# One load of the rotary weights ahead of the next phase's weights, and two weightings moved ahead of the step sizes at three sequences

## The chip, the cores and the metric

The kernel runs on one core of a Trainium2 chip. The time is that of the device, in microseconds (us), from one launch to its end; the median of several runs counts. A profiled execution gives the trace and has a time of its own.

## The reference, cut to what matters

The program is a decoder of four layers over `x` of 16 sequences, 128 rows each, 256 wide, all in float32. Each layer has a mixer or attention, a cross attention and a feed-forward part, each on a layer norm of `x` and added to `x`. Two of the twelve parts are touched.

The mixer of layer 2 (a state-space scan, 32 heads of 16, state 128):

```python
gate, hBC, dt = jnp.split(hidden @ in_proj_w.T, [INTER, INTER + CONV_DIM], axis=-1)
hBC = silu(causal_conv4(hBC, conv_w) + conv_b)
xs, B, C = jnp.split(hBC, [INTER, INTER + STATE], axis=-1)
dt = clip(softplus(dt + dt_bias), 0, 100)
# per head, causal: y[l] = sum over s <= l of
#     (C[l] . B[s]) * exp(sum of A*dt over s+1..l) * (dt[s] * xs[s])   + D * xs[l]
y = y * silu(gate)
return (y * rsqrt(mean(y * y) + EPS) * norm_w) @ out_proj_w.T
```

The cross attention of layer 2 (latent, 16 heads, 64 rotary columns each):

```python
kv_c, q_c = kv @ W_kvc, q @ W_dq
q_nope, q_rope = q_c @ W_uq, rope(q_c @ W_qr)
k_nope, k_rope, v = kv_c @ W_uk, rope(kv_c @ W_kr), kv_c @ W_uv
scores = (q_nope . k_nope + q_rope . k_rope) * scale, masked by seg_id
return softmax(scores) @ v @ W_o
```

`rope` swaps the two halves of the 64 columns for its second term, so the kernel keeps `W_qr` twice: as it is, and with the halves of each head swapped.

## The kernel before, in words

The twelve parts are phases that run one after another. Each phase is one or two blocks; a block has a program for each engine (`block.sync` for SP, which issues the loads, `block.gpsimd`, `block.tensor`, `block.scalar`, `block.vector`), and all engines meet at its end. Within a block the order on each engine is written out by hand, and engines wait for each other by semaphores. Weights of the next phase go into the other half of an arena `w`: the function `after(sp)`, made by `load_next`, issues them at the start of a phase.

**The mixer** (`mixer`, L1663; called for both layers with a mixer, with `PADDED` true only for the larger one of layer 2) treats the 16 sequences in 4 groups of 4 (`TG`). The vector engine's loop over sequences `q` weights the decays: `weigh(d)` (L2007, instruction at L2011) multiplies a tile of 8 heads x 128 x 128 decay factors by the similarity `gm`. In the larger mixer there are `PT` = 4 such tiles for a sequence, made in two pairs (`PU` = 2) by ScalarE's `decay` (L1860, an Exp at L1865), which waits for `exponents` on TensorE. TensorE's `outputs` (L2216) takes the weighted tiles one by one. `add(q)` (L2027) adds the projected result of the sequence before, `gated(q)` (L2022) takes the gate, `values(q)` (L1998) makes the scaled inputs. The work of the next group is woven in: after sequence `t` = 0 of a group come `step_bias` (L1939, adds the bias to the step-size product, then frees its PSUM bank), ScalarE's `softplus` (L1837 to L1841), two convolutions (`conv`, L1981; ScalarE's copies ahead of them at L1830 and L1832), and after `t` = 1 `step_sizes` (L1947 and behind). Products of that kind take turns in two PSUM banks, so the second convolution's product takes the bank that the step-size product had. These are the lines of the order before, on VectorE around a sequence with `t` = 0:

```python
for i in range(PT):
    weigh(PT * q + i)
    if q >= 1 and i == PU - 1:
        add(q - 1)
```

**The latent preparation** (`phase_xattn2`, L2819, first block) multiplies out the per-head weights on TensorE (L2914, L2919; ScalarE copies them out at L2932, L2935), normalises the first group, and splits the rotary weights into a rounded part `wh` (ScalarE, L2938) and the rest `wl` (VectorE, L2965). The split weights have three kinds of rows, `LAT`, `ROPE` and `SWAP`. SP issues, in this order: the next phase's weights (`in_l2f_up`, `in_l2f_down`), three copies of `in_l2x_qr` into `raw` (as it is, and each half into the place of the other), the segment numbers `seg`, and the first context tile. ScalarE and VectorE wait for all four small loads together, with one semaphore. The second block begins with TensorE's L3170 (which wants the context tile) and ScalarE's L3012 (which wants the next phase's weights).

## Time and profile before

| | |
|---|---|
| median of 3 runs | 2321.14 us (2319.14 to 2321.93) |
| the profiled execution | 2322.72 us, span 2320.9 us |
| mean granted TensorE clock | 0.947 |
| busy: TensorE, VectorE, ScalarE, GpSimd | 89%, 69%, 53%, 13% |
| loads `in_l2f_up`, `in_l2f_down` | 2048 KB and 1024 KB |
| loads `in_l2x_qr`: full, two halves | 384 KB, 192 KB each |
| loads `seg`, context tile | 8 KB, 512 KB |

The span runs from the first to the last instruction. A timeline line gives the start in us from the span's start, the duration in us of what was merged in the line, engine, line of the kernel, operation, output <- inputs, and in brackets how long the engine sat idle before it and what ended that. The granted clock is a share of 2.4 GHz: 1.00 is 2.4 and 0.50 is 1.2. Matmuls overlap each other, so that starts tell more of them than durations.

### The profile page before, as it was taken

Reading aid. Unit: us, or ns where it says so; the run is one execution under the profiler, and the core shown is the slowest. Engines: PE = TensorE matmul, PEld = TensorE weight load, DVE = VectorE, ACT = ScalarE, POOL = GpSimd, SP = SyncE. Lnnn points to the kernel's source line nnn. Section 1 sums busy time; section 2 is a strip of 40 time slices with the busy share of each in tenths; the row PEclk is TensorE's granted clock in tenths of the full one; section 3 lists DMA queues with packets and bytes.
Section 4 is the critical chain, followed back from the end, with each engine's and each line's share of the span. In section 5 each row is a group of like instructions: output and inputs, shape, how many; then the busy total and the mean of one; then the engine's idle time right before and its main releaser. Section 6 shows DMA issues by size and latency. Waiting matters only on the chain. (4 is left out here: it accounts for less than half of the span.)

```text
span 2320.9 us, 46693 instructions
## 1 busy us (share of the span) xinstructions
PE 2065.3 (89%) x18816; PEld 1575.8 (68%) x18816; DVE 1601.7 (69%) x2974; ACT 1237.4 (53%) x2455; POOL 302.0 (13%) x307
## 2 busy tenths in 40 slices
PE   7978989899899898888879898979889879999996
PEld 4644458677555787556657666758656658999996
DVE  5756657676465897777858877857566676766763
ACT  2325664544466444555546456565478524665663
POOL 0010000011310000001000000000100113444432
PEclk9978999899999999899989999999899879999998
DMA  3020010100100002000020000010200035666663
GB/s 120 22 66 23 14 44 1 37 1 1 60 20 24 12 1 72 1 1 1 1 78 10 9 18 0 0 37 1 73 2 2 7 120 184 207 193 221 197 206 89
DMA packets 62793, 126.10 MB, mean 54 GB/s; under 512 B 16073, under 2 KB 45386, under 8 KB 62442
## 3 DMA queue, kind: packets, MB, share of 16 engines
q1 hardware_dynamic: 53770, 111.35, 14.3%
q0 software_dynamic: 8832, 12.06, 2.6%
q8 instruction: 137, 2.24, 0.4%
q14 instruction: 54, 0.43, 0.1%
HBM read 109.18 MB, written 15.80 MB: 54 GB/s over the span
## 5 line engine op out<-in xcount | busy, mean ns | idle before, releaser
L268 PE MATMUL ps<-ffn_xh,ffn_wh 128*128 128x256 f32 x644 | 184.0, 286 | 1.5 <-DVE ffn_xl L4379 1.5
L268 PE MATMUL ps<-ffn_xh,ffn_wl 128*128 128x256 f32 x644 | 182.4, 283 | 0.0
L268 PE MATMUL ps<-ffn_xl,ffn_wh 128*128 128x256 f32 x644 | 182.3, 283 | 0.0
L4374 DVE TENSOR_TENSOR ffn_wl<-ffn_fresh,ffn_wh 128x1792 fp32r<-128x1792 f32 x69 | 139.5, 2024 | 26.4 <-ACT ffn_wh L4254 26.4
L216 POOL TENSOR_TENSOR all_rstd<-all_mv,all_cst 128x4 f32<-128x4 f32 x40 | 8.4, 210 | 1063.6 <-DVE all_mv L194 1063.6
L1981 DVE SCALAR_TENSOR_TENSOR attn_xc<-attn_cx,all_w,attn_xc 128x512 f32<-128x512 f32 (+1 forms) x144 | 107.3, 749 | 48.2 <-ACT attn_xc L1832 44.7
L268 PEld LDWEIGHTS ps<-ffn_xh,ffn_wh 128*128 128x128 f32 x644 | 123.5, 192 | 1.7 <-DVE ffn_xl L4379 1.7
L4254 ACT ACTIVATE ffn_wh<-ffn_fresh 128x1792 fp32r<-128x1792 f32 x69 | 117.0, 1695 | 14.4 <-DMA ffn_fresh<-in_l3f_w 14.4
L268 PEld LDWEIGHTS ps<-ffn_xl,ffn_wh 128*128 128x128 f32 x644 | 123.4, 192 | 0.0
L268 PEld LDWEIGHTS ps<-ffn_xh,ffn_wl 128*128 128x128 f32 x644 | 123.4, 192 | 0.0
L3028 ACT ACTIVATE xattn_sc<-xattn_sc,xattn_mx 128x128 f32<-128x128 f32 x256 | 98.8, 392 | 17.7 <-DVE xattn_mx L3126 17.7
L4241 POOL DMA_INDIRECT x_acc<-ffn_y,ffn_row_i x46 | 78.8, 1713 | 215.6 <-ACT ffn_y L4282 197.9
L268 PE MATMUL ps<-ffn_wh,ffn_hh 128*128 128x256 f32 x322 | 94.2, 293 | 3.9 <-DVE ffn_hl L4387 3.9
L1203 PE MATMUL ps<-ffn_xh,ffn_w 128*128 128x512 f32 x224 | 90.3, 403 | 7.9 <-ACT ffn_w L3312 3.8
L2011 DVE TENSOR_TENSOR attn_e<-attn_e,all_w 128x1024 f32<-128x1024 f32 (+1 forms) x80 | 86.6, 1116 | 14.0 <-ACT attn_e L1865 12.7
L260 PE MATMUL ps<-all_xnT,all_w 128*128 128x512 f32 (+1 forms) x176 | 90.5, 645 | 4.3 <-ACT all_xnT L772 2.6
L268 PE MATMUL ps<-ffn_wl,ffn_hh 128*128 128x256 f32 x322 | 91.1, 283 | 0.0
L268 PE MATMUL ps<-ffn_wh,ffn_hl 128*128 128x256 f32 x322 | 91.0, 283 | 0.0
L1203 PE MATMUL ps<-ffn_xl,ffn_w 128*128 128x512 f32 x224 | 89.4, 399 | 0.0
L4397 DVE TENSOR_TENSOR all_xnT<-ps,all_xn 128x512 f32<-128x512 f32 x92 | 57.2, 622 | 41.4 <-PE ps L268 38.4
L254 PE MATMUL ps<-all_cst 128*128 128x512 f32 x102 | 58.1, 721 | 30.6 <-ACT attn_zs L1852 11.3
L2401 ACT ACTIVATE xattn_pT<-ps 128x1024 f32<-128x1024 f32 x64 | 62.0, 1021 | 40.7 <-PE ps L2511 40.2
(483 smaller groups left out, 6079.4 us busy)
## 6 DMA issues: line engine op xcount, KB each, us to landing
ffn_fresh<-in_l3f_w SPq DMA_DIRECT2D x69, 896.0 KB, 4.9
all_w<-in_ctxT SPq DMA_DIRECT2D x12, 512.0 KB, 5.7
all_w<-in_ctx SPq DMA_DIRECT2D x8, 512.0 KB, 6.7
all_x<-in_x_rows SPq DMA_DIRECT2D x4, 512.0 KB, 7.3
all_x<-x_seq SPq DMA_DIRECT2D x4, 512.0 KB, 5.4
all_w<-in_l2x_o SPq DMA_DIRECT2D x1, 2048.0 KB, 9.3
all_w<-in_l2f_up SPq DMA_DIRECT2D x1, 2048.0 KB, 8.4
xattn_ctxT<-in_ctxT SPq DMA_DIRECT2D x4, 512.0 KB, 3.7
```

Of the source, the lines that this page charges most:

```text
L254: pe.matmul(k.psum[bank][:, :], k.c["ident"], k.cst[:, 0:512], start=True, stop=True)
L260: last = pe.matmul(out, w[:, c, n0:n1], k.xnT[:, c, a:b], start=start and c == 0, stop=stop and c == KC - 1)
L268: last = pe.matmul(out, a, b, start=start and n == 0, stop=stop and n == 2)
L1203: last = pe.matmul(out, w[:, c, f * P:(f + 1) * P], part[:, c, :], start=c == 0 and n == 0, stop=c == KC - 1 and n == 1)
L1981: ins = dve.scalar_tensor_tensor(out, cx[0:n, c % 2, :, j:j + P], tap, out, ALU.mult, ALU.add)
L2011: dve.tensor_tensor(e[:, d % SLOTS_E], e[:, d % SLOTS_E], gm[:, q % 2].unsqueeze(1).broadcast_to([P, HP, P]), ALU.mult).then_inc(m_ready.s ...
L2401: act.activation(pT[:, m % 2, 2 * half:2 * half + 2].rearrange("p j c q -> p j (c q)"), k.ps[:, 2 * half:2 * half + 2, :], ACT.Exp, scale= ...
L3028: last = act.activation(s, s, ACT.Exp, bias=mx[:, n % nS, e, h:h + 1], scale=-1.0, accum_out=total[:, n % nS, e, h:h + 1])
L4241: pool.indirect_dma_start(acc[:, :], bass.IndirectOffsetOnAxis(ap=row_i[:, at:at + 1], axis=0), y[:, j % 2, v, :], None, compute_op=ALU.ad ...
L4254: act.activation(wh[:, j % 2, piece(q)], fresh[:, piece(q)], ACT.Copy).then_inc(high_ready.sem, 1)
L4374: dve.tensor_tensor(wl[:, j % 2, piece(q)], fresh[:, piece(q)], wh[:, j % 2, piece(q)].bitcast(F32), ALU.subtract).then_inc(low_ready.sem, 1)
L4397: dve.tensor_tensor(h[:, n % 2, 0:width], B[n % 2][:, 0:width], sa[:, n % 2, 0:width], ALU.mult).then_inc(h_ready.sem, 1)
```

## The change

In the larger mixer, at the sequences with `t` = 0 of the first three groups (0, 4 and 8), the first two weightings of the next sequence are written right behind `values(q + 1)`, ahead of `step_bias`; the next turn of the loop leaves them out. In the latent preparation there is one load of the rotary weights in place of three, and it, the segment numbers and the context tile are issued ahead of the next phase's weights. The swapped halves are made from the one copy, by two roundings and two subtractions over 96 x 16 x 32 elements in place of one each over 96 x 1024.

```diff
+            def early(q):
+                return PADDED and q % TG == 0 and q // TG < last_group
+
...
+                first_weighed = q >= 1 and early(q - 1)
                 for i in range(PT):
-                    weigh(PT * q + i)
+                    if not (first_weighed and i < PU):
+                        weigh(PT * q + i)
                     if q >= 1 and i == PU - 1:
                         add(q - 1)
...
                 gated(q)
                 if q + 1 < BATCH:
                     values(q + 1)
+                if early(q):
+                    for i in range(PU):
+                        weigh(PT * (q + 1) + i)
                 if more and t == 0:
                     step_bias(g)
...
-        raw = qL[0:MQ, 0:4, :].rearrange("p a t -> p (a t)").rearrange("p (s h r) -> p s h r", s=2, h=MH)
+        raw = qL[0:MQ, 0:2, :].rearrange("p a t -> p (a t)").rearrange("p (h r) -> p h r", h=MH)
+        def by_head(a, s):
+            return a[:, s].rearrange("p a b -> p (a b)").rearrange("p (h r) -> p h r", h=MH)
...
-                after(sp)
-                qr = k.ins["l2x_qr"].rearrange("c (h r) -> c h r", h=MH)
-                sp.dma_start(raw[:, 0], qr).then_inc(small.sem, 16)
-                sp.dma_start(raw[:, 1, :, 0:half], qr[:, :, half:MR]).then_inc(small.sem, 16)
-                sp.dma_start(raw[:, 1, :, half:MR], qr[:, :, 0:half]).then_inc(small.sem, 16)
+                sp.dma_start(raw[:, :, :], k.ins["l2x_qr"].rearrange("c (h r) -> c h r", h=MH)).then_inc(small.sem, 16)
                 sp.dma_start(seg_i[:, :], k.ins["seg"]).then_inc(small.sem, 16)
                 sp.dma_start(ctxT[:, :, :], sources_xattn1(k)[1][0]).then_inc(ctx_loaded.sem, 16)
-                sp.wait_ge(*small(0, 64))
+                after(sp)
+                sp.wait_ge(*small(0, 32))
...
-                act.wait_ge(*small(0, 64))
-                for s in range(2):
-                    act.activation(wh[:, ROPE + s].rearrange("p a b -> p (a b)"),
-                                   raw[:, s].rearrange("p h r -> p (h r)"), ACT.Copy).then_inc(rounded.sem, 1)
+                act.wait_ge(*small(0, 32))
+                act.activation(by_head(wh, ROPE), raw[:, :, :], ACT.Copy).then_inc(rounded.sem, 1)
+                act.activation(by_head(wh, SWAP)[:, :, 0:half], raw[:, :, half:MR], ACT.Copy).then_inc(rounded.sem, 1)
+                act.activation(by_head(wh, SWAP)[:, :, half:MR], raw[:, :, 0:half], ACT.Copy).then_inc(rounded.sem, 1)
...
-                dve.wait_ge(*small(0, 64))
+                dve.wait_ge(*small(0, 32))
                 dve.tensor_copy(seg_f[:, :, 0], seg_i[:, :])
-                for s in range(2):
-                    dve.wait_ge(*rounded(0, s + 1))
-                    dve.tensor_tensor(wl[:, ROPE + s].rearrange("p a b -> p (a b)"), raw[:, s].rearrange("p h r -> p (h r)"),
-                                      wh[:, ROPE + s].rearrange("p a b -> p (a b)").bitcast(F32), ALU.subtract)
+                dve.wait_ge(*rounded(0, 1))
+                dve.tensor_tensor(by_head(wl, ROPE), raw[:, :, :], by_head(wh, ROPE).bitcast(F32), ALU.subtract)
+                dve.wait_ge(*rounded(0, 3))
+                for a, b in ((slice(0, half), slice(half, MR)), (slice(half, MR), slice(0, half))):
+                    dve.tensor_tensor(by_head(wl, SWAP)[:, :, a], raw[:, :, b], by_head(wh, SWAP)[:, :, a].bitcast(F32), ALU.subtract)
```

VectorE in the mixer around sequence 8, the kernel before (`attn_e` are the decays, L2022 is `gated(8)`, L1998 `values(9)`, L1939 the bias add, L1981 convolutions, L2027 `add(8)`):

```order
L2022 TENSOR_TENSOR all_xnT<-ps,attn_zs 128x512
L1998 TENSOR_TENSOR all_w<-ps,all_w 128x16x16 x2
L1939 TENSOR_TENSOR all_w<-ps,all_w 128x128
L1981 SCALAR_TENSOR_TENSOR attn_xc<-attn_cx,all_w,attn_xc 128x512 x6
L2011 TENSOR_TENSOR attn_e<-attn_e,all_w 128x1024 x2
L2027 SCALAR_TENSOR_TENSOR all_x<-ps,attn_ss,all_x 128x256
L2011 TENSOR_TENSOR attn_e<-attn_e,all_w 128x1024 x2
```

And in the changed kernel:

```order
L2022 TENSOR_TENSOR all_xnT<-ps,attn_zs 128x512
L1998 TENSOR_TENSOR all_w<-ps,all_w 128x16x16 x2
L2011 TENSOR_TENSOR attn_e<-attn_e,all_w 128x1024 x2
L1939 TENSOR_TENSOR all_w<-ps,all_w 128x128
L1981 SCALAR_TENSOR_TENSOR attn_xc<-attn_cx,all_w,attn_xc 128x512 x6
L2027 SCALAR_TENSOR_TENSOR all_x<-ps,attn_ss,all_x 128x256
L2011 TENSOR_TENSOR attn_e<-attn_e,all_w 128x1024 x2
```

The first of the two pairs now stands ahead of the bias add, and `add` stands directly behind the convolutions.

SP in the latent preparation, before (L303 are the next phase's weights):

```order
L303 DMA all_w<-in_l2f_up 128x16x256
L303 DMA all_w<-in_l2f_down 128x2x1024
L2892 DMA xattn_qL<-in_l2x_qr 96x1024
L2893 DMA xattn_qL<-in_l2x_qr 96x16x32
L2894 DMA xattn_qL<-in_l2x_qr 96x16x32
L2895 DMA xattn_seg_i<-in_seg 128x16
L2896 DMA xattn_ctxT<-in_ctxT 128x2x512
```

And in the changed kernel:

```order
L2901 DMA xattn_qL<-in_l2x_qr 96x1024
L2902 DMA xattn_seg_i<-in_seg 128x16
L2903 DMA xattn_ctxT<-in_ctxT 128x2x512
L4562 ISA
L303 DMA all_w<-in_l2f_up 128x16x256
L303 DMA all_w<-in_l2f_down 128x2x1024
```

The small loads now stand ahead of both large ones, and the two copies in pieces of 32 elements are gone.

## Rows read from the trace of the kernel before

**Rows 1.** Busy time by stretch: length, each engine, then PEclk, DMA share, GB/s

```profile
907.00:1191.00 284.00, 240.87 (x2108) 171.75 (x2108) 216.35 (x339) 155.59 (x256) 26.95 (x41) 0.95 0.06 16
1098.00:1104.00 6.00, 6.00 (x16) 4.84 (x17) 1.66 (x3) 1.23 (x3) 0.00 (x0) 0.50 0.00 0
1191.00:1211.00 20.00, 11.51 (x73) 7.70 (x74) 8.30 (x28) 8.16 (x17) 1.22 (x2) 0.72 0.77 225
```

**Rows 2.** Timeline of VectorE after sequence 8: start, us, instruction, [idle before it]

```profile
1094.88 0.75 DVE L1998 TENSOR_TENSOR all_w<-ps,all_w 128x256 f32<-128x256 f32 x2
1098.64 0.29 DVE L1939 TENSOR_TENSOR all_w<-ps,all_w 128x128 f32<-128x128 f32 x1 [3.01 <-PE ps L268]
1102.60 2.33 DVE L1981 SCALAR_TENSOR_TENSOR attn_xc<-attn_cx,all_w,attn_xc 128x512 f32<-128x512 f32 x3 [3.67 <-ACT attn_xc L1832]
...
1107.40 2.35 DVE L2011 TENSOR_TENSOR attn_e<-attn_e,all_w 128x1024 f32<-128x1024 f32 x2
...
1110.06 2.35 DVE L2011 TENSOR_TENSOR attn_e<-attn_e,all_w 128x1024 f32<-128x1024 f32 x2
1112.33 2.32 DVE L1981 SCALAR_TENSOR_TENSOR attn_xc<-attn_cx,all_w,attn_xc 128x512 f32<-128x512 f32 x3
```

**Rows 3.** Timeline of ScalarE: the decays after sequences 0, 4 and 8

```profile
971.02 1.94 ACT L1865 ACTIVATE attn_e<-ps 128x1024 f32<-128x1024 f32 x2
...
1028.15 1.93 ACT L1865 ACTIVATE attn_e<-ps 128x1024 f32<-128x1024 f32 x2
...
1036.74 1.94 ACT L1865 ACTIVATE attn_e<-ps 128x1024 f32<-128x1024 f32 x2
...
1095.69 1.93 ACT L1865 ACTIVATE attn_e<-ps 128x1024 f32<-128x1024 f32 x2
...
1107.44 1.94 ACT L1865 ACTIVATE attn_e<-ps 128x1024 f32<-128x1024 f32 x2
```

**Rows 4.** Timeline of TensorE: second convolution after 4, outputs after 8

```profile
1031.96 0.39 PE L268 MATMUL ps<-attn_xh,attn_win_high 128*128 128x512 f32 x1
...
1109.82 1.08 PE L2216 MATMUL ps<-attn_e,all_w 128*32 128x128 f32 x32
1111.33 0.64 PE L2216 MATMUL ps<-attn_e,all_w 128*32 128x128 f32 x16 [0.43 <-DVE attn_e L2011]
1112.47 0.65 PE L2216 MATMUL ps<-attn_e,all_w 128*32 128x128 f32 x16 [0.49 <-DVE attn_e L2011]
```

**Rows 5.** Timeline of VectorE after sequences 0 and 4

```profile
971.07 2.35 DVE L2011 TENSOR_TENSOR attn_e<-attn_e,all_w 128x1024 f32<-128x1024 f32 x2
...
1030.68 0.29 DVE L1939 TENSOR_TENSOR all_w<-ps,all_w 128x128 f32<-128x128 f32 x1 [2.60 <-PE ps L268]
...
1037.85 2.35 DVE L2011 TENSOR_TENSOR attn_e<-attn_e,all_w 128x1024 f32<-128x1024 f32 x2
```

**Rows 6.** Timeline of SP's DMA issues in the latent preparation

```profile
1194.53 1.27 SPq L2892 DMA_DIRECT2D xattn_qL<-in_l2x_qr  x1
...
1200.88 4.27 SPq L2895 DMA_DIRECT2D xattn_seg_i<-in_seg  x1
```

**Rows 7.** Timeline of ScalarE in the latent preparation

```profile
1203.30 0.82 ACT L2935 ACTIVATE xattn_wvo<-ps 128x256 f32<-128x256 f32 x2 [0.32 <-PE ps L2919]
1206.62 2.00 ACT L2938 ACTIVATE xattn_wh<-xattn_qL 96x1024 fp32r<-96x1024 f32 x2 [2.51 <-DMA xattn_seg_i<-in_seg]
```

**Rows 8.** Timeline of VectorE in the latent preparation

```profile
1206.62 0.17 DVE L2962 CAST xattn_seg_f<-xattn_seg_i 128x16 f32<-128x16 int32 x1 [8.35 <-DMA xattn_seg_i<-in_seg]
1207.71 2.36 DVE L2965 TENSOR_TENSOR xattn_wl<-xattn_qL,xattn_wh 96x1024 fp32r<-96x1024 f32 x2 [0.91 <-ACT xattn_wh L2938]
```

**Rows 9.** Timeline of TensorE at the latent block's end and after

```profile
1200.33 3.36 PE L2919 MATMUL ps<-all_w 128*64 128x256 f32 x24
1210.70 3.42 PE L3170 MATMUL ps<-xattn_ctxT,xattn_wkv 128*128 128x512 f32 x4 [7.02 <-DVEq L3058]
1213.96 1.88 PE L260 MATMUL ps<-all_xnT,all_w 128*96 128x512 f32 x4
```

## The prediction

> **What bounds the kernel now.** Time before is a median of 2321.14 us; the profiled execution took 2322.72 us, of which 2320.9 us is the span. I sum against the profiled execution and shift the result by the difference of 1.58 us. A reading of no change is within 0.2% of the median, 4.6 us; that is about what a measurement of this kernel can resolve.
>
> The first view is the busy time by stretch [rows 1]. In the larger mixer, 907 to 1191 us, TensorE is busy 240.87 of 284 us and VectorE 216.35: both are near their limit and neither is always the bound. The 20 us behind it, the weight preparation of the latent attention, are different: TensorE is busy 11.51 us, VectorE 8.30, ScalarE 8.16, and DMA has a share of 0.77.
>
> Next, the timelines around the places that the change names. After sequence 8, VectorE finishes `values` (L1998) at 1095.63, waits 3.01 us for TensorE's step-size product, does the 0.29 us bias add (L1939), waits 3.67 us for the convolution input, does two convolutions, and only at 1107.40 starts weighting the decays of sequence 9 (L2011) [rows 2]. ScalarE had begun these two decays at 1095.69 and was done in 1.93 us [rows 3]. So work of 2.27 us that could be done in an idle gap is done in a full stretch. Behind 1107.40 VectorE has no wait: pair, add, pair, convolution. TensorE is the one who waits there, 0.43 and 0.49 us, for the weighted decays [rows 4]. Sequences 0 and 4 look alike: the late pairs start at 971.07 and 1037.85 [rows 5].
>
> Last, the latent preparation. SP issues the next phase's weights, then three copies of the rotary weights, then the segment numbers. The segment numbers, last of these, are issued only at 1200.88, and the issue alone takes 4.27 us [rows 6]. ScalarE is done with its product copies at 1204.12 and then waits 2.51 us for that last load [rows 7]. VectorE waits 8.35 us for it and ends with its two subtractions at 1210.07 [rows 8]. TensorE is done at 1203.69, waits 7.02 us and starts the next block at 1210.70 [rows 9]: 0.63 us behind VectorE's end. This join is what sets the end of the stretch, since every engine must reach it.
>
> **The change, part by part: the mixer.** It moves two weightings at each of three sequences (after 0, 4 and 8), and adds or removes none.
>
> *After sequence 8.* The first moved weighting can start when the first decay is out: 1095.69 and half of the pair's 1.93 with a little tail is about 1096.75. The pair takes 2.35 us [rows 2], so it ends at 1099.1. Behind it on VectorE's queue stands the bias add, now at 1099.1 in place of 1098.64: 0.5 us late. What waits for it is ScalarE's softplus, which in its order stands behind the inverse of the norm and runs just ahead of 1107.44, and the bank for TensorE's second next product. Neither is due for over 2 us, and the next convolution starts at 1102.60 as before. The cost is nothing, and the cover is the 3.67 us wait.
>
> At 1107.40 the pair is gone and the add comes first. Add and pair together took 1110.06 - 1107.40 = 2.66, the pair 2.27, so the add 0.4: done at 1107.8. The second pair now has a wait that was hidden: ScalarE's decays 3 and 4 start at 1107.44 [rows 3], the first out at 1108.45. The pair runs 1108.5 to 1110.8; before, the next convolution began at 1112.33. Gain **1.55 us**. 0.7 us of the 2.27 is lost to that new wait.
>
> *After sequence 0.* Old start 971.07, decays from 971.02 [rows 3, 5], so the second pair runs 972.05 to 974.35, where it used to end 4.93 us after 971.07 (the same row of work as 1107.40 to 1112.33), at 976.00. Gain **1.65 us**.
>
> *After sequence 4.* Old start 1037.85, but the decays begin at 1036.74, so the first is out at 1037.75 and there is no new wait. All of the pair is won: **2.27 us**. Here TensorE's product comes earlier, at 1030.68 [rows 5]. The decays start at 1028.15 [rows 3], the moved pair runs 1029.2 to 1031.5 and the bias add ends at 1031.8, 0.8 us late. The product that reuses its bank starts at 1031.96 [rows 4]; I take **0.1 us** for a late free, between 0 and 0.3.
>
> Does TensorE follow? Its own path is full from the step-size products to the first outputs, which start at 1109.82 [rows 4]. It then finds the first two weightings long ready, the third at 1109.7 and the fourth at 1110.9: it wins its two waits and a little of overlap, 1.1 us, and hands over the next transposes that much earlier. VectorE then is the one with no idle, so I take its 1.55. Between TensorE's waits of 0.92 and VectorE's 1.55 this is the open size of the term. For the mixer: 1.65 + 2.27 + 1.55 - 0.1 = **5.4 us**, with 2.8 us if TensorE's two waits alone count at each of the three.
>
> **The latent preparation.** One copy of 96 x 1024 elements goes first, then the segment numbers and the context, and then the next phase's weights. The first issue costs what it did, 1.27 us [rows 6]; the other two are gone. The block starts near 1191.8, so the small loads are under way by 1194.5 instead of 1200.88, almost 10 us before ScalarE wants them at 1204.12. The waits of 2.51 and 8.35 us go; what is late next is ScalarE itself, with the copies before it. From 1204.1: the full rounding 1.04 us (two took 2.00, [rows 7]); then the two half-row roundings, 512 elements each, some 0.55 us each (half of 1.00 and a fixed part), so 1205.1 and 1206.3. VectorE subtracts the full part from 1205.2 (1.2 us, [rows 8]) to 1206.4 and the two halves by 1207.6 or 1207.7 at 0.65 each. It ended at 1210.07. Gain **2.4 us**; between 1.9, if each small instruction has 0.15 us more of fixed time, and 2.7.
>
> The added wait is on the other side. 3 MB of the next phase's weights are issued some 2.5 us later, behind 0.9 MB. ScalarE's first instruction of the next block wants them. Of before I know that the DMA share over these 20 us was 0.77 at 225 GB/s [rows 1]; at this mean rate, which holds idle time too, 4.0 MB from 1192 end at 1209.8, against a new block start of 1208.3. But ScalarE only converts 1.48 us of ternary weights there and its first urgent copy is over 3 us behind the block's start, so I take 0, and up to 1.5 as the bound. Here the Trainium skill (DMA: Bandwidth & Descriptors, Rules for kernel authors) speaks against the change: issue a transfer early and wait late, and this edit issues the largest one later. By that rule taken alone the 1.5 us above would be lost and the latent term would be 0.9. No row shows it yet.
>
> The sum is 5.4 + 2.4 = 7.8 us: 2322.72 - 7.8 = 2314.9 for the profiled execution, **2313.3** for the median.
>
> **The clock.** TensorE's granted clock was 0.50 (1.2 GHz) from 1098 to 1104, though TensorE was busy all of these 6 us [rows 1]; after sequence 4 the same convolution products ran at 2.4 GHz. Six busy us at half the clock cost at most 3 us. The mean in the mixer is 0.95. At the latent's second block four product halves took 3.42 us while four of the same width just behind took 1.88 [rows 9]: the restart after the 7.02 us of idle ran at 1.2 GHz. I expect that idle to be 4.6 us and the restart as slow as now. A restart at 2.4 GHz would give 1.5 us more and a median of 2311.8. The Trainium skill (TensorE: Matmul & The Clock Gate, Why this matters for your kernels) warns of idle gaps between bursts of matmuls as what drops the clock; the row of 3.42 us agrees, and by that rule a gap that is shorter but still there may win nothing of this.
>
> **The rivals.**
>
> *TensorE is the mixer's bound.* For it: no wait on it before 1109.82. Against it: it waits behind, and VectorE doesn't. Mixer 2.8, latent 2.4, so 5.2 in all: 2315.9.
>
> *The mixer's gain is given back* in the group's later sequences, where VectorE waits for ScalarE's silu and convolution copies. Against it: these follow VectorE's own gated product, so they move along. Then only 2.4 us are left: 2318.7.
>
> *The load was not what held the latent block*, or the weights behind it come late by the rule above: 5.4 to 6.3 us are left, 2314.8 to 2315.7.
>
> *Slower: the clock.* One mechanism, anywhere in the mixer or behind it, because all later work shifts against the stretches at 1.2 GHz. Each costs up to 3 us by [rows 1]. From three stretches more than now the 7.8 us are eaten, from five the kernel is slower by over 0.2%: 2321.14 - 7.8 + 15 = 2328. Denser products behind each early sequence speak against more of them; one fewer is as likely, and gives 2310.3.
>
> **How the numbers follow.** The sum as forecast: 0.52. TensorE as the bound: 0.16. Late weights: 0.08. Mixer given back: 0.08. One or two slow stretches fewer, or the faster restart: 0.12. Slower or equal by the clock: 0.04. The first three and the fifth, 0.88 together, lie beyond 0.2% (below 2316.5); 0.08 of them I give to no change for the scatter of single runs (2319.14 to 2321.93 before), as some are within 1 or 2 us of that bound. So faster 0.80, same 0.17, slower 0.03. The range 2309.0 to 2318.0 takes in one slow stretch less, and 2.4 us alone but for its last 0.7.
>
> **What would show it.** In the changed profile: the group L2011 starts within 1.2 us of `values` after sequences 0, 4 and 8; the bias add has no idle before it; the second pair behind has an idle of about 0.7 us for ScalarE after 0 and 8 and none after 4; TensorE's waits of 0.43 and 0.49 there are gone. The mixer takes some 278.6 us and not 284. In the latent block ScalarE and VectorE wait for no DMA, the block from mixer's end to TensorE's restart takes 2.4 us less, and ScalarE's ternary copy starts without a wait. It would be wrong if ScalarE waits there for DMA beyond the next block's first product, if TensorE waits for the bank of the bias add, or if the mean clock of the whole span (0.947) moves by 0.003 or more, which alone is up to 7 us.

## The result, and the profile after

The changed kernel takes 2308.95 us (median of 9 runs, 2303.51 to 2313.37) against 2320.01 us of the kernel before (9 runs, 2315.01 to 2323.27). The ratio is 0.9952, with a 95% interval of 0.9941 to 0.9963: 11.1 us less, between 8.6 and 13.7. The forecast was 7.8 us less and 2313.3 us. The direction holds; the time is 0.05 us under the range's low end of 2309.0, so that it fell outside and not inside is luck. What was wrong is the size of the mixer's term, as the parts below show. A few executions took over 3000 us, whatever the kernel, and count in no ratio; one of them is among the eight of `e11`, whose median is 2318.94 us with it and 2318.28 without.

The profiled execution took 2306.32 us. From its page, the span, the busy times and the clock:

```profile
span 2304.5 us, 46693 instructions
...
PE 2055.2 (89%) x18816; PEld 1569.9 (68%) x18816; DVE 1600.1 (69%) x2975; ACT 1238.0 (54%) x2456; POOL 302.9 (13%) x307
```

The mean granted clock is 0.952 (0.947 before). Since one profiled pair differs by 16.4 us and the medians by 11.1, the difference has to be cut into parts before it is read. The cuts are points of the program that both kernels have: the gated product (L2022 before) of sequence 0 and of sequence 15 in the larger mixer, TensorE's first product of the second latent block, and ScalarE's first copy of `xattn_qL` behind it. Times are read on VectorE, TensorE and ScalarE from the span's start; the span itself is known to 0.1 us.

| stretch | before | after | difference |
|---|---|---|---|
| start to gated(0), code not touched | 957.77 | 952.93 | -4.84 |
| gated(0) to gated(15) | 229.45 | 218.62 | -10.83 |
| gated(15) to the restart of TensorE | 23.48 | 21.01 | -2.47 |
| restart to the first `qL` copy | 11.46 | 12.77 | +1.31 |
| from there to the end, code not touched | 1098.7 | 1099.2 | +0.4 |

Two of five parts hold no edit, and one of them differs by 4.8 us: untouched code varies that much between two executions. The part with the mixer's edit is double its forecast, the latent block is as forecast, and the piece behind it gives half back.

The mixer by intervals, from the busy times by stretch: gated(0) to gated(15), then gated(0) to gated(1), gated(4) to (5) and gated(8) to (9). The columns are those of [rows 1]: length, TensorE, its weight loads, VectorE, ScalarE, GpSimd, granted clock, DMA share, GB/s. Before:

```profile
957.77:1187.22 229.45, 201.34 (x1870) 144.46 (x1868) 177.56 (x271) 125.72 (x205) 20.65 (x34) 0.96 0.01 1
957.77:978.24 20.47, 19.45 (x150) 14.65 (x148) 13.17 (x19) 9.22 (x17) 1.18 (x2) 0.83 0.01 2
1026.73:1045.03 18.30, 16.44 (x145) 12.40 (x143) 13.09 (x19) 9.21 (x17) 1.19 (x2) 0.94 0.00 1
1094.27:1114.57 20.30, 19.38 (x150) 14.59 (x147) 13.18 (x19) 9.22 (x17) 1.19 (x2) 0.83 0.00 1
```

And after:

```profile
952.93:1171.55 218.62, 196.81 (x1870) 141.93 (x1868) 177.28 (x270) 125.80 (x205) 20.71 (x34) 0.97 0.01 1
952.93:969.03 16.10, 16.09 (x150) 12.17 (x148) 13.10 (x18) 9.22 (x17) 1.20 (x2) 1.00 0.01 2
1017.54:1033.57 16.03, 16.03 (x150) 12.11 (x147) 13.10 (x19) 9.22 (x17) 1.20 (x2) 1.00 0.00 1
1082.48:1098.52 16.04, 16.04 (x150) 12.12 (x147) 13.10 (x19) 9.23 (x17) 1.19 (x2) 1.00 0.01 2
```

The three intervals got shorter by 4.37, 2.27 and 4.26 us, 10.9 in all: the whole difference of the mixer. All three now take 16.03 to 16.10 us at full clock, and TensorE is busy in all of it: 16.03 of 16.03 us. Before, it was busy 16.44 of 18.30 between 4 and 5, so it idled for 1.86 us in one interval, twice the 0.92 of [rows 4]. These are three waits ahead of weighted tiles:

```profile
1040.26 0.65 PE L2216 MATMUL ps<-attn_e,all_w 128*32 128x128 f32 x16 [0.49 <-DVE attn_e L2011]
1041.79 0.65 PE L2216 MATMUL ps<-attn_e,all_w 128*32 128x128 f32 x16 [0.88 <-DVE attn_e L2011]
1042.93 1.08 PE L2216 MATMUL ps<-attn_e,all_w 128*32 128x128 f32 x16 [0.49 <-DVE attn_e L2011]
```

After sequence 8 the slow clock had made TensorE itself late, and only 0.43 and 0.49 us were left of them. The two intervals with a clock of 0.83 shrank by 2 us more than the one with 0.94.

VectorE after sequence 8, with the columns of [rows 2] (L2011 is still the weighting):

```profile
1085.02 2.37 DVE L2011 TENSOR_TENSOR attn_e<-attn_e,all_w 128x1024 f32<-128x1024 f32 x2 [1.19 <-ACT attn_e L1865]
1087.32 0.28 DVE L1939 TENSOR_TENSOR all_w<-ps,all_w 128x128 f32<-128x128 f32 x1
1089.14 4.56 DVE L1981 SCALAR_TENSOR_TENSOR attn_xc<-attn_cx,all_w,attn_xc 128x512 f32<-128x512 f32 x6 [1.54 <-ACT attn_xc L1832]
1093.62 0.48 DVE L2027 SCALAR_TENSOR_TENSOR all_x<-ps,attn_ss,all_x 128x256 f32<-128x256 f32 x1
1094.01 2.35 DVE L2011 TENSOR_TENSOR attn_e<-attn_e,all_w 128x1024 f32<-128x1024 f32 x2
```

The moved pair starts 1.19 us behind `values`, and the bias add follows it with no idle. Where waits of 3.01 and 3.67 us stood [rows 2], 1.19 and 1.54 are left. The second pair, at 1094.01, has no wait, where the forecast had 0.7 us. ScalarE made its decays from 1092.60, 1.4 us ahead of it:

```profile
1092.60 1.94 ACT L1865 ACTIVATE attn_e<-ps 128x1024 f32<-128x1024 f32 x2
```

TensorE then takes all four weighted tiles in one piece, without the two waits of [rows 4]:

```profile
1094.95 2.11 PE L2224 MATMUL ps<-attn_e,all_w 128*32 128x128 f32 x64
```

The latent preparation, SP's issues:

```profile
1176.01 0.35 SPq L2901 DMA_DIRECT2D xattn_qL<-in_l2x_qr  x1
1176.40 0.42 SPq L2902 DMA_DIRECT2D xattn_seg_i<-in_seg  x1
...
1177.93 5.68 SPq L303 DMA_DIRECT2D all_w<-in_l2f_down  x1
```

The segment numbers are issued 0.4 us behind the start in 0.42 us, where they took 4.27 [rows 6]. The long issue has moved to `in_l2f_down`, with nobody behind it. ScalarE:

```profile
1188.42 1.04 ACT L2945 ACTIVATE xattn_wh<-xattn_qL 96x1024 fp32r<-96x1024 f32 x1
1189.37 0.62 ACT L2946 ACTIVATE xattn_wh<-xattn_qL 96x512 fp32r<-96x512 f32 x1
...
1192.46 1.48 ACT L3021 ACTIVATE xattn_ternary_w<-all_w 128x1536 bf16 x1 [1.95 <-DVEq L3068]
```

There is no wait for a DMA ahead of the roundings, where 2.51 us stood [rows 7]. The ternary copy, which wants the weights now issued later, waited 1.95 us for the end of the block and for no load. TensorE's restart:

```profile
1192.56 3.78 PE L3179 MATMUL ps<-xattn_ctxT,xattn_wkv 128*128 128x512 f32 x4 [4.46 <-DVEq L3067]
1196.13 2.88 PE L260 MATMUL ps<-all_xnT,all_w 128*96 128x512 f32 x4
```

Its idle is 4.46 us, not 7.02 [rows 9], and this too is as forecast (4.6). But the four products of the forecast's 1.88 us now take 2.88, and those ahead 3.78 and not 3.42.

### The profile page after: what moved, and what is told of

Same layout as the page of the kernel before. It is cut to its first block and busy times, and to the rows that moved or that the text cites. A ratio compares the mean times of both kernels' runs of the same rounds, so it can differ in the third digit from the quotient of the medians.

```text
span 2304.5 us, 46693 instructions
## 1 busy us (share of the span) xinstructions
PE 2055.2 (89%) x18816; PEld 1569.9 (68%) x18816; DVE 1600.1 (69%) x2975; ACT 1238.0 (54%) x2456; POOL 302.9 (13%) x307
## 5 line engine op out<-in xcount | busy, mean ns | idle before, releaser
L1981 DVE SCALAR_TENSOR_TENSOR attn_xc<-attn_cx,all_w,attn_xc 128x512 f32<-128x512 f32 (+1 forms) x144 | 107.0, 749 | 40.2 <-ACT attn_xc L1832 36.8
L2011 DVE TENSOR_TENSOR attn_e<-attn_e,all_w 128x1024 f32<-128x1024 f32 (+1 forms) x80 | 86.6, 1116 | 17.6 <-ACT attn_e L1865 16.3
```

Source lines behind the costliest of these rows:

```text
L1981: ins = dve.scalar_tensor_tensor(out, cx[0:n, c % 2, :, j:j + P], tap, out, ALU.mult, ALU.add)
L2011: dve.tensor_tensor(e[:, d % SLOTS_E], e[:, d % SLOTS_E], gm[:, q % 2].unsqueeze(1).broadcast_to([P, HP, P]), ALU.mult).then_inc(m_ready.s ...
```

## The experiments

Three questions are open: which part gave the time, why the mixer gave twice its forecast, and what held the latent block and what took back its gain.

### Each part alone

The mixer's edit alone (`e1_mixer_only`; as a diff of the changed kernel, the latent block goes back to the text before):

```diff
-                sp.dma_start(raw[:, :, :], k.ins["l2x_qr"].rearrange("c (h r) -> c h r", h=MH)).then_inc(small.sem, 16)
+                after(sp)
+                qr = k.ins["l2x_qr"].rearrange("c (h r) -> c h r", h=MH)
+                sp.dma_start(raw[:, 0], qr).then_inc(small.sem, 16)
...
```

> The mixer's edit alone; the latent preparation as before. Theory A (the change moves work only, and the clock's slow stretches fall in either kernel with the same chance): VectorE wins 2.27 us after a sequence where TensorE runs at 2.4 GHz and about 1.6 where it runs at 1.2 GHz, so the three give 4.8 to 6.8 us and the time is 2313 to 2315 against a before of 2320. Theory B (the denser outputs of TensorE behind each early sequence also keep the clock up): 8 to 9 us, 2311 to 2312, and in the profile no slow stretch between the gated products after sequences 0, 4 and 8. In both, the interval between these gated products is 16.0 us wherever the clock is full in it.

Measured: 2309.65 us (2306.62 to 2315.05), ratio 0.9957 [0.9941, 0.9972], so 10.0 us less.

```profile
955.44:1174.02 218.58, 196.76 (x1870) 141.95 (x1868) 177.25 (x270) 125.71 (x205) 20.64 (x34) 0.97 0.01 1
```

This row of the busy times by stretch, gated(0) to gated(15), agrees with the changed kernel's to 0.04 us. The three intervals take 16.11, 16.04 and 16.02. Its latent pieces, with the text of before, are gated(15) to the restart and the restart to the first `qL` copy:

```profile
1174.02:1198.07 24.05, 13.69 (x82) 9.21 (x83) 8.93 (x28) 8.97 (x20) 2.40 (x4) 0.77 0.65 187
1198.07:1211.03 12.96, 12.67 (x38) 6.90 (x39) 7.22 (x15) 2.95 (x4) 0.00 (x0) 0.77 0.14 41
```

The latent edit alone (`e2_latent_only`, against the changed kernel):

```diff
             def early(q):
-                return PADDED and q % TG == 0 and q // TG < last_group
+                return False
```

> The latent edit alone; the mixer's order as before. The block from the mixer's last gated product to TensorE's restart takes 21.0 us and not 23.5, so 2.4 us are won: 2317.6 against 2320. Theory A: nothing more. A rival, that the latent edit carries the excess of the result through the clock behind it (restart after a shorter idle at 2.4 GHz): 5 to 6 us, 2314.5. In the mixer, the intervals after sequences 0, 4 and 8 are 18.3 us where the clock is full and about 20.4 where it is slow.

Measured: 2319.76 us (2313.01 to 2324.33), ratio 1.0002 [0.9991, 1.0013]: 0 us, with 2.6 either way. So nearly all of the result is the mixer's; the 2.4 us that were expected of the latent edit alone don't show in the total. Its mixer, with the text of the kernel before, gives a second look at the late order, gated(0) to (15), (4) to (5) and (8) to (9):

```profile
957.58:1185.82 228.24, 201.23 (x1870) 143.84 (x1868) 177.32 (x270) 126.01 (x205) 20.70 (x34) 0.96 0.01 1
1025.19:1045.02 19.83, 17.99 (x150) 13.32 (x147) 13.08 (x19) 9.23 (x17) 1.20 (x2) 0.91 0.00 1
1093.92:1112.22 18.30, 16.44 (x150) 12.08 (x147) 13.08 (x19) 9.22 (x17) 1.20 (x2) 1.00 0.01 1
```

The interval of sequence 8 ran at full clock this time and took 18.30 us, 2.26 more than 16.04. The one of sequence 4 was disturbed in its turn. After sequence 0 the late order ran at full clock in `e11`, an experiment below:

```profile
954.95:973.31 18.36, 16.50 (x150) 12.12 (x148) 13.07 (x18) 9.22 (x17) 1.19 (x2) 1.00 0.00 1
```

That is 2.26 more than the 16.10 of the changed kernel. For sequence 4 no trace of the late order has a clock of 1.00; at 0.94 it took the same 18.30, 2.27 more than 16.03. So undisturbed, the move is worth the whole pair, 2.27 us, after every one of the three.

### Is the rest of the mixer's gain the clock?

The late order and the early order were each run with one and with two more `idle_products` ahead of the larger mixer's first work. These are meant to change where in time the mixer lies and leave its order alone. `e5_late_delayed` is the latent edit alone, `e6_early_delayed` the changed kernel, both with:

```diff
-            idle_products(pe, k, 0, 3)
+            idle_products(pe, k, 0, 5 if PADDED else 3)
             exponents(0)
```

> The latent-only kernel with two more idle products on TensorE ahead of the larger mixer's first sequence, so that all of its 16 sequences start 1.7 to 3.4 us later. Read from the first gated product to the last: 228.2 us without the delay. Theory A (where the slow stretches fall against the sequences is a matter of position, and this sets what the late order costs beyond the moved work): the pattern of slow stretches changes and the interval changes with it by 1 us or more, to anything from 225.5 to 230. Theory B (the late order itself causes slow stretches): the same 228.2 within 0.3.

> The full change with the same delay. Without it, first to last gated product is 218.6 us. Theory A: this too changes by 1 us or more, and the difference to the late order with the same delay comes out anywhere between 6.8 us (three times 2.27) and 11. Theory B: 218.6 within 0.3, and the difference to the late order stays 9.6.

`e11_late_delayed_less` and `e12_early_delayed_less` have 4 in place of 5:

```diff
-            idle_products(pe, k, 0, 3)
+            idle_products(pe, k, 0, 4 if PADDED else 3)
             exponents(0)
```

> The late order (latent-only kernel) with one more idle product ahead of the mixer's first sequence, for a third position of the slow stretches. First to last gated product so far 229.4, 228.2 and 229.6 us; expected within 227 to 231. It is for the mean cost of the late order over positions.

> The early order (full change) with the same one more idle product. So far 218.6 and 220.4 us; expected within 218 to 221. If the moved work alone counted, the mean over positions would be 6.8 us under the late order's; I expect 8.5 to 10, the excess because the late order has the longer path and the pauses on which slow stretches fall.

Measured, with ratios against the kernel before on the same chip:

| idle products | late order | early order | mixer late | mixer early | difference |
|---|---|---|---|---|---|
| 3 | `e2` 1.0002 [0.9991, 1.0013] | after 0.9952 [0.9941, 0.9963] | 228.24 | 218.62 | 9.62 |
| 4 | `e11` 0.9993 [0.9980, 1.0007] | `e12` 0.9969 [0.9954, 0.9984] | 227.12 | 217.84 | 9.28 |
| 5 | `e5` 1.0016 [1.0004, 1.0028] | `e6` 0.9981 [0.9969, 0.9993] | 229.62 | 220.35 | 9.27 |

The mixer columns are gated(0) to gated(15) in the traces. With 4 idle products gated(0) falls at the same time in both orders, 954.95 and 954.99; in the other two pairs it is 1.5 and 4.7 us apart, so the pair with 4 is the cleanest. Late with 4 and with 5, then early with 4 and with 5:

```profile
954.95:1182.07 227.12, 199.61 (x1870) 142.79 (x1868) 177.37 (x271) 125.90 (x205) 20.68 (x34) 0.96 0.00 1
```

```profile
955.92:1185.54 229.62, 199.95 (x1870) 142.94 (x1868) 177.24 (x270) 125.68 (x205) 20.69 (x34) 0.96 0.00 1
```

```profile
954.99:1172.83 217.84, 191.54 (x1870) 137.04 (x1868) 177.33 (x270) 125.49 (x205) 20.65 (x34) 1.00 0.01 1
```

```profile
957.46:1177.81 220.35, 195.55 (x1870) 141.09 (x1868) 177.39 (x270) 125.48 (x205) 20.62 (x34) 0.98 0.00 1
```

`e12` is the useful one: a whole mixer at a clock of 1.00, in 217.84 us. Three times 2.27 us on top give 224.6 us for the late order at full clock. Against these two, the early order's traces lose 0 to 2.5 us to the clock (217.84 to 220.35), the late order's 2.5 to 5.0 (227.12 to 229.62, with the 229.45 of the kernel before among them). So with the same number of idle products the early order wins 9.3 to 9.6 us: 6.8 of moved work and 2.5 to 2.8 of clock. The position alone moves either order by 2.5 us, as much as the clock term itself. Even without a shift a mixer can vary: the kernel before and `e3` below are the same program up to the end of the mixer and take 229.45 and 228.18. Added up from rows of half a microsecond, TensorE ran at 1.2 GHz for 17.0 to 20.5 us in the six mixers of the late order (before, `e2` to `e5`, `e11`) and for 0 to 13.7 us in the five of the early order (after, `e1`, `e6`, `e8`, `e12`). So the sign of the clock term rests on all of them; its size is uncertain by a microsecond or so. `e5` and `e6` moved by over 1 us each, as the theory of mere position asked, and the difference stayed near 9.3, where the other theory had 9.6 and the first anything from 6.8 to 11: position and order both count.

The totals follow this less closely than the traces. By the ratios, late less early is 11.6 us with 3 idle products, 5.6 with 4 and 8.1 with 5, each with some 4 to 5 us of uncertainty. In the pair with 4 the mixer's 9.28 us do not reach the total of the profiled executions (2318.28 and 2313.23): behind layer 3's first gate load, where nothing is edited, `e12` took 490.8 us at a clock of 0.92 and `e11` 486.9 at 0.94. In microseconds the medians are 2318.94 (`e11`), 2313.09 (`e12`), 2321.94 (`e5`) and 2312.59 (`e6`). The traces are one execution each.

In `e10_late_filled` the latent edit alone has products of 256 columns added at two places among the outputs of the sequences with `t` = 1, where TensorE pauses for VectorE in the late order. Their result is not used.

```diff
                     outputs(PT * q + i)
+                    if PADDED and q % TG == 1 and q // TG < last_group and i in (1, 2):
+                        later_jobs.wait_free(pe, ("rows", q + 1))
+                        pe.matmul(later_jobs.bank(("rows", q + 1))[:, 0:256], k.c["ident"], k.cst[:, 0:256], start=True, stop=True)
```

> The latent-only kernel, its mixer in the late order, but TensorE's waits between the outputs of sequences 1, 5 and 9 are filled with one product of 256 columns each into a free bank; its result is used by nobody. If these pauses are what drops the clock, the slow stretch at 16.5 us behind the first gated product is gone and the first two intervals take what they do at full clock: the mixer takes 227.4 us or less where it took 228.2. If only the position counts, the stretch stays and the mixer takes 228.2 to 229 us.

Measured: 2318.53 us, ratio 0.9994 [0.9981, 1.0007].

```profile
957.13:1185.04 227.91, 203.45 (x1882) 144.58 (x1880) 177.29 (x271) 125.67 (x205) 20.69 (x34) 0.96 0.01 1
```

The stretch at 1.2 GHz that `e2` has 16.5 us behind gated(0), just behind those pauses, is gone: gated(0) to gated(2) takes 32.40 us and not 33.15. But later ones fell on the intervals of 4 and 8 (19.27 and 19.67 us at 0.91), and the mixer is only 0.3 us shorter than in `e2`, where 0.8 or more was expected if pauses are the cause. That speaks for those pauses as what brought this one on, though the filler also shifts what follows, and it left waits of 0.49 and 0.26 us among these outputs. It did not give back the 2.5 us. The slow stretch of [rows 1], 1098 to 1104, lies on products without a pause, and the one after sequence 0 in the same trace began 3.3 us behind gated(0), where nothing on TensorE is moved yet. Neither is explained by the waits that the change takes away. Why the early order has less time at 1.2 GHz stays open.

### One pair more

`e7_also_third` moves the pair after the sequences with `t` = 2 too (2, 6 and 10):

```diff
             def early(q):
-                return PADDED and q % TG == 0 and q // TG < last_group
+                return PADDED and q % TG in (0, 2) and q // TG < last_group
```

> The full change, and the first two weightings are moved ahead after sequences 2, 6 and 10 too, into VectorE's wait of 3.1 us ahead of the last convolution. The decays are out about 1.1 us into that wait, so the pair ends some 0.35 us after the convolution could start: 1.9 us are won at each of the three where VectorE is the bound behind it, 5.7 us in all, 2303 against a before of 2320. The rival: behind these sequences TensorE's sums, and not VectorE, set the next group, and the 0.35 us late is lost three times: 2310.

Measured: 2304.43 us (2302.55 to 2308.82), ratio 0.9941 [0.9928, 0.9955]. It ran on another chip than the changed kernel, where the kernel before takes 2317.75 us, so only the ratios compare.

```profile
957.64:1174.87 217.23, 196.43 (x1870) 142.44 (x1868) 177.57 (x271) 125.13 (x205) 20.66 (x34) 0.97 0.00 1
...
1021.27:1038.48 17.21, 17.21 (x150) 13.39 (x147) 13.19 (x18) 9.21 (x17) 1.18 (x2) 0.90 0.00 1
```

gated(2) to gated(3) falls from 17.47 to 15.50 us, and the next interval grows from 17.00 to 17.98: half of the gain is given back one sequence later. That is neither the 1.9 us at each that was expected nor the rival's loss. Three times the remaining 1.0 are 3 us, but slow stretches now lie on the convolution products of 4 and 8 (17.21 us, not 16.03), and the mixer wins only 1.4 us. By the ratios, 0.9941 and 0.9952, the totals are 2.6 us apart, with overlapping intervals.

### The latent block: order, number, and who rounds

`e3_three_first` keeps the three copies and the two roundings of the kernel before and only moves the large weights behind the small loads:

```diff
-                after(sp)
                 qr = k.ins["l2x_qr"].rearrange("c (h r) -> c h r", h=MH)
...
                 sp.dma_start(ctxT[:, :, :], sources_xattn1(k)[1][0]).then_inc(ctx_loaded.sem, 16)
+                after(sp)
```

> Latent part only, order alone: the three copies of before, the segment numbers and the context are issued ahead of the next phase's weights, and still rounded and subtracted in two instructions each. If the place in the queue is what counts, all have landed before ScalarE's last product copy, the waits for DMA are gone, and the gain is 2.3 to 2.6 us. If it is the copies in pieces of 128 bytes that are slow, they land late in this place too, and the gain is under 1 us.

Measured: 2319.58 us (2311.88 to 2330.1), ratio 1.0003 [0.9988, 1.0018]. `e4_one_behind` is `e2` with one load, behind the large weights:

```diff
+                after(sp)
                 sp.dma_start(raw[:, :, :], k.ins["l2x_qr"].rearrange("c (h r) -> c h r", h=MH)).then_inc(small.sem, 16)
...
-                after(sp)
```

> Latent part only, number alone: one load of the rotary weights, but behind the next phase's weights as before. If the place in the queue is what counts, the segment numbers still land after ScalarE's last product copy and a wait of 1 to 2.5 us stays on ScalarE, gain 0 to 1.3 us. If the two copies in pieces are what held the queue, the segment numbers land some 5 us earlier and the gain is 2.4 us as with the full edit.

Measured: 2314.25 us (2311.74 to 2319.74), ratio 0.9976 [0.9964, 0.9989]. The totals say little here; the blocks do. gated(15) to the restart, `e3` and `e4`:

```profile
1181.03:1202.23 21.20, 13.87 (x83) 9.27 (x83) 8.92 (x28) 8.76 (x19) 2.40 (x4) 0.82 0.67 202
```

```profile
1187.72:1210.26 22.54, 13.93 (x83) 9.29 (x83) 8.99 (x29) 9.09 (x21) 2.41 (x4) 0.80 0.56 182
```

With `e2`'s 21.26 us and 23.48 before, the order alone wins all of it (21.20), and the number alone 0.9 us. In `e4`, SP's issue of the segment numbers takes 0.43 us and not 4.27, but ScalarE still waits 1.16 us for that load, since it stands behind 3 MB:

```profile
1196.38 0.43 SPq L2903 DMA_DIRECT2D xattn_seg_i<-in_seg  x1
...
1206.11 1.06 ACT L2945 ACTIVATE xattn_wh<-xattn_qL 96x1024 fp32r<-96x1024 f32 x1 [1.16 <-DMA xattn_seg_i<-in_seg]
```

In `e3` the copies in small pieces stand ahead of the large weights and hold these up instead. The weights' first issue comes 6.3 us behind the first small one (1191.83 and 1185.49), where it comes 1.5 us behind in the changed kernel, and the next block's ternary copy waits for them.

```profile
1204.00 1.48 ACT L3012 ACTIVATE xattn_ternary_w<-all_w 128x1536 bf16 x1 [3.86 <-DMA all_w<-in_l2f_down]
```

That is the price that the rule on early issues spoke of, and the piece behind it shows next to nothing of it: its restart to first `qL` copy takes 13.02 us against 12.94 in `e2`. The 5 us that the total of `e4` is lower do not come from this block, though; the last part of the experiments takes them up.

`e8_vector_rounds` takes the three roundings from ScalarE, which is behind with its copies, and gives them to VectorE, which idled for 6.82 us:

```diff
-                act.wait_ge(*small(0, 32))
-                act.activation(by_head(wh, ROPE), raw[:, :, :], ACT.Copy).then_inc(rounded.sem, 1)
-                act.activation(by_head(wh, SWAP)[:, :, 0:half], raw[:, :, half:MR], ACT.Copy).then_inc(rounded.sem, 1)
-                act.activation(by_head(wh, SWAP)[:, :, half:MR], raw[:, :, 0:half], ACT.Copy).then_inc(rounded.sem, 1)
...
                 dve.tensor_copy(seg_f[:, :, 0], seg_i[:, :])
+                dve.tensor_copy(by_head(wh, ROPE), raw[:, :, :]).then_inc(rounded.sem, 1)
+                dve.tensor_copy(by_head(wh, SWAP)[:, :, 0:half], raw[:, :, half:MR]).then_inc(rounded.sem, 1)
+                dve.tensor_copy(by_head(wh, SWAP)[:, :, half:MR], raw[:, :, 0:half]).then_inc(rounded.sem, 1)
```

> The full change, and the three roundings of the rotary weights are made by VectorE, which idles 6.8 us there, and not by ScalarE. The block then ends with ScalarE's last product copy: 21.0 us from the last gated product to TensorE's restart become 17.7. If the clock's restart costs what it does now, 3.3 us are won; if the idle of about 1 us that is left no longer drops the clock, the restart runs at 2.4 GHz and 2.5 us more are won, 2303 in all. The rival: the slow stretch falls on the restart whatever the idle, and gives nothing more.

Measured: 2298.46 us (2296.35 to 2300.99), ratio 0.9913 [0.9899, 0.9927], the best of all versions: some 20 us below the kernel before by the ratio (19.3 by the medians, 2317.75 on this chip), and its interval lies below that of the changed kernel. gated(15) to the restart, restart to the first `qL` copy; then VectorE, ScalarE and TensorE from its timelines:

```profile
1175.79:1193.41 17.62, 13.69 (x83) 9.21 (x83) 10.08 (x32) 6.87 (x17) 2.41 (x4) 0.81 0.63 216
1193.41:1203.43 10.02, 9.73 (x38) 5.93 (x39) 7.23 (x15) 2.83 (x4) 0.00 (x0) 1.00 0.23 82
```

```profile
1186.84 0.68 DVE L2967 CAST xattn_wh<-xattn_qL 96x1024 fp32r<-96x1024 f32 x1
...
1195.89 1.48 ACT L3020 ACTIVATE xattn_ternary_w<-all_w 128x1536 bf16 x1 [3.12 <-DMA all_w<-in_l2f_down]
...
1193.41 1.98 PE L3178 MATMUL ps<-xattn_ctxT,xattn_wkv 128*128 128x512 f32 x4 [1.07 <-DVEq L3066]
1195.22 1.88 PE L260 MATMUL ps<-all_xnT,all_w 128*96 128x512 f32 x4
```

Here the full rounding takes 0.68 us, 1.04 on ScalarE. TensorE idles for 1.07 us only and restarts at full clock: 1.98 and 1.88 us for the two groups, where the changed kernel has 3.78 and 2.88. The two pieces take 27.64 us together against 33.78: 3.4 us by the work and 2.75 by the clock. The next phase's weights are late here, 3.12 us for ScalarE, and TensorE is still busy for 9.73 of the 10.02 us. So the restart at full clock, which was one of the two expectations, came true, and `e9` repeats it behind the same 1.07 us of idle.

`e9_all_three` joins this with the third moved pair:

```diff
             def early(q):
-                return PADDED and q % TG == 0 and q // TG < last_group
+                return PADDED and q % TG in (0, 2) and q // TG < last_group
...
                 dve.tensor_copy(seg_f[:, :, 0], seg_i[:, :])
+                dve.tensor_copy(by_head(wh, ROPE), raw[:, :, :]).then_inc(rounded.sem, 1)
...
```

> The full change with both additions: weightings ahead after sequences 2, 6 and 10 too, and VectorE's rounding of the rotary weights. If the two are independent, 9 us of the second and 1 to 2 of the first add up: 2297 against a before of 2318, better than either. The mixer from first to last gated product is between 213.6 us, if no slow stretch falls on the convolution products behind sequences 4 and 8, and 217.2, if one falls on each as in the run with the third sequences.

Measured: 2303.16 us (2299.48 to 2307.35), ratio 0.9929 [0.9912, 0.9947], where 2297 us were expected: 3.7 us slower than `e8` alone by the ratios, with overlapping intervals. Its mixer takes 217.21 us, its latent pieces 18.16 and 10.02, as in `e7` and `e8` but for 0.5 us ahead of the restart. What it lost lies elsewhere.

### A stretch that nobody edited

From the load of the next attention's first tables to layer 3's first gate load, the work is the same in all kernels. `e8` and `e9`:

```profile
1513.27:1812.20 298.93, 263.85 (x2380) 197.31 (x2380) 192.09 (x389) 197.69 (x463) 16.50 (x24) 0.98 0.07 22
```

```profile
1511.48:1815.70 304.22, 270.19 (x2380) 202.36 (x2380) 192.34 (x389) 197.85 (x463) 16.55 (x24) 0.95 0.06 21
```

It comes out in two kinds: 298.6 to 299.1 us at a clock of 0.97 or 0.98 (`e4`, `e7`, `e8`) and 302.5 to 304.2 at 0.95 (before, after and the other nine). That can make up to 5 us of a total with no edit in it: more than the 2.3 us by which the profiled executions of `e8` and `e9` differ, and perhaps the excess of `e4`, whose latent block had won only 1. For `e4` it isn't shown: its profiled execution, with the short kind, took 2319.74 us and was the slowest of its ten. It is one trace of each kernel, so whether a kernel always gets the same kind wasn't tested.

## Why the prediction was wrong

**The mixer's size, the step that failed.** The forecast was 1.65 + 2.27 + 1.55 - 0.1 = 5.4 us; the traces show 9.3 to 9.6 with the same number of idle products and 10.8 for the profiled pair. Two errors add up.

The first is the 0.7 us taken off after sequences 0 and 8, "that new wait" for the decays. It was read from [rows 2, 3] as if the decays at 1107.44 were due then in any case. But they were late because TensorE ran at 1.2 GHz ahead of them [rows 1]; at full clock they start 1.4 us before VectorE wants them. So it is 2.27 us three times, 6.8 in place of 5.5. I had the counterexample in hand, sequence 4, and treated it as another case where it was the undisturbed one. That step is shown: the moved pair of sequence 8 is followed by one without a wait, and `e2` and `e11` give 2.26 us after 8 and 0.

The second is the clock, held as it stood in one execution and named only as a rival of one stretch fewer, with 0.12 for this and the faster restart together. With 3, 4 and 5 idle products the early order lost 2.5 to 2.8 us less to it. That this is near the forecast's 3 us for a stretch is luck: the slow stretches in the intervals of 0 and 8 cost 2.1 and 2.0 each (20.47 for 18.36 and 20.30 for 18.30), and in `e6` three of them cost 2.5 together. The forecast's own sign of being wrong came true as well, a mean clock that moves by 0.003 or more: it went from 0.947 to 0.952. Why the early order has less time in slow stretches is not settled (in `e6` they do fall on its convolution products): `e10` points to the pauses for one of them, and leaves the others.

**TensorE as the bound** was priced at 0.92 us a sequence from the two waits of sequence 8. That is the same error once more: at the undisturbed sequence 4 there are three, 1.86 us together. The rival's 2.8 us fell. But with these waits gone TensorE is busy in all of the changed interval (16.03 of 16.03 us), so no wait for VectorE is left to win in it. The bank was right in size: after sequence 4 the second convolution's first product took 0.49 us in place of 0.39 and the next one followed by 0.33 in place of 0.23, the 0.1 us of the forecast; that the bank is the cause isn't shown. The gain was not given back in the later sequences.

**The latent block** was forecast at 2.4 us less and came out at 2.47, with the loads early, no wait for DMA and an idle of 4.46 us where 4.6 stood. Its half roundings took 0.62 us and not 0.55. Wrong is what came behind: "the restart as slow as now". The slow stretch at the restart begins some 19.7 us behind gated(15) in both traces (1206.8 and 1191.3), while TensorE is idle. Before, TensorE stood idle through more than half of it, at no cost; now it restarts 2.5 us earlier, into the same stretch, and 1.3 us go back. The two pieces together are 34.94 us before and 33.78 after. `e1`, with the latent text of before, has 37.01 (24.05 and 12.96), so the position moves this too: `e1` restarts behind 7.50 us of idle and is as slow as the changed kernel, `e7` restarts behind 4.46 us and takes only 11.45. That the shorter idle is what gives part of the gain back is thus a reading of one pair. The edit is worth 0.7 (`e2` against before) to 3.2 us (after against `e1`) by the traces compared. As a total it was measured at 0, with 2.6 either way.

The 1.5 us for late weights were rightly not taken. The Trainium skill (DMA: Bandwidth & Descriptors, Rules for kernel authors) wants transfers issued early; `in_l2f_down` came up to 3.86 us late for ScalarE (`e3`) and the piece behind it grew by under 0.1 us (13.02 for 12.94). The 1.5 us for a restart at full clock was too low: `e8` shows 2.75. The Trainium skill's warning on idle gaps (TensorE: Matmul & The Clock Gate, Why this matters for your kernels) agrees with the restarts: slow behind 7.02 and 4.46 us of idle, fast behind 1.07. The stretches that begin in dense products, as the one 3.3 us behind gated(0), are not of that kind.

**The sum:** +4.0 in the mixer with the same number of idle products, and -1.3 or more behind the latent block, give 10.5 for 7.8; 11.1 was measured, 8.6 to 13.7. The low end of the range took in one slow stretch, not a mis-sized term and the clock at once.

## What to carry to other kernels

Before a wait or a duration goes into a sum, look at the granted clock of its stretch, and take the price from the occurrence that ran at full clock; a wait that only shows at 1.2 GHz is no cost of the new order. TensorE's idle time at the slow clock costs nothing, so shortening it can hand part of the gain back; closing it nearly (here by giving three small roundings to the idle engine, 6.1 us in these two pieces) won the clock as well, in two traces of two. With a clock that shifts untouched stretches by up to 5 us, compare intervals between fixed points of the program, the same edit at several positions, and totals by their ratios on one chip, not one pair of totals.

## What the runs showed of the hardware

- TensorE's granted clock is not set by the work at hand alone: the same mixer text took 228.18 to 229.45 us in four traces, 227.12 and 229.62 with its start shifted, and the same attention took 299 or up to 304 us. It fell to 1.2 GHz inside work in which TensorE was busy 6.00 of 6.00 us [rows 1] as well as in its idle time.
- An issue on SP can block for long: 4.27 us for 8 KB behind 3 MB and two copies in pieces of 32 elements, 0.43 us for the same 8 KB behind the same 3 MB and one copy in whole rows (`e4`), 3.29 us behind the same two copies with no 3 MB ahead (`e3`), 5.68 us for `in_l2f_down` once it came last. What stands behind such an issue pays, not what it loads.
- VectorE rounds 96x1024 elements to fp32r in 0.68 us, ScalarE in 1.04.
